# The causal clearing of the attention's diagonal blocks, moved from VectorE's product with a triangle to POOL's select on partition and position

## What is computed

```python
q, k, v = (split_heads(_layernorm(x) @ W + b) for W, b in qkv)   # (B, 16, T, 8)
scores = (l2norm(q) @ l2norm(k).T) * SCALE / TEMP
scores = where(tril(ones(T, T)), scores, -inf)                    # causal
x = x + 0.5 * (softmax(scores) @ v).merge() @ Wo + ...
```

## Time and profile before

| | us |
|---|---|
| median of 3 runs (lowest to highest) | 1459.83 (1456.45 to 1460.56) |
| the profiled execution's own time | 1460.59 |
| its span, first to last instruction | 1458.7 |
| PE / DVE / ACT / POOL busy | 1172.2 / 1118.2 / 804.6 / 659.2 |
| the attention: first to last exponential begins | 983.0 to 1426.0 |

### The profile page before, as it was taken

The page is one execution under the profiler, slowest core; times in us unless marked ns, Lnnn a source line. Parts: engine busy times, 40 slices in busy tenths (PEclk is TensorE's granted clock), DMA queues, the critical chain, the costliest instruction groups (busy, mean ns, idle before and its releaser), DMA issues. The chain is left out here.

```text
span 1458.7 us, 33100 instructions
## 1 busy us (share of the span) xinstructions
PE 1172.2 (80%) x11444; PEld 747.4 (51%) x11444; DVE 1118.2 (77%) x2557; ACT 804.6 (55%) x1477; POOL 659.2 (45%) x859
## 2 busy tenths in 40 slices
PE   7679954798898988998739994558987998899894
PEld 7369953455454545554618993444443543443333
DVE  6959963878888888899687995567778878876644
ACT  3768845455145235311347883127876777677881
POOL 2366633753773674365347663353233431521100
PEclk6789985698888898898658997568998999998996
DMA  9035340000000000000502342000000000000000
GB/s 283 11 99 171 89 59 15 26 5 5 20 9 1 23 9 2 2 2 2 197 4 77 90 89 44 15 15 14 2 23 6 19 23 1 16 8 8 1 16 8
DMA packets 55715, 55.11 MB, mean 38 GB/s; under 512 B 9882, under 2 KB 44484, under 8 KB 55556
## 3 DMA queue, kind: packets, MB, share of 16 engines
q1 hardware_dynamic: 46468, 34.37, 7.6%
q0 software_dynamic: 9088, 18.63, 5.7%
HBM read 32.26 MB, written 20.71 MB: 36 GB/s over the span
## 5 line engine op out<-in xcount | busy, mean ns | idle before, releaser
L2137 ACT ACTIVATE l_probs<-l_ps 128x1024 f32<-128x1024 f32 (+1 forms) x320 | 288.0, 946 | 106.6 <-PE l_ps L2023 104.7
L781 POOL DMA_INDIRECT ffn_yg<-y_rows,ffn_index x156 | 156.8, 1005 | 81.5 <-PE ffn_ps_t L796 37.8
L2042 PE MATMUL l_ps<-l_probs,l_vs 128*32 128x512 f32 (+3 forms) x1536 | 167.2, 525 | 28.0 <-DVE l_oTs L2370 16.2
L864 ACT ACTIVATE ffn_hT<-ffn_ps_h,experts_b1T,experts_scales 128x256 f32<-128x256 f32 x312 | 150.8, 562 | 30.5 <-PE ffn_ps_h L811 29.0
L263 POOL DMA_INDIRECT combine_og<-o_rows,combine_place x128 | 139.9, 1093 | 53.8 <-issue 31.4
L1307 PE MATMUL ssm_ps<-ssm_X,ssm_near 32*32 32x256 f32 x2048 | 136.8, 418 | 1.6 <-DVE ssm_Y L1750 1.6
L2361 DVE TENSOR_TENSOR l_probs<-l_probs,last_tri 128x256 f32<-128x256 f32 x256 | 102.5, 438 | 43.0 <-ACT l_probs L2137 41.2
L2023 PE MATMUL l_ps<-l_qkT 32*128 32x512 f16 (+3 forms) x768 | 110.6, 342 | 17.5 <-ACT l_probs L2137 15.4
L889 DVE SCALAR_TENSOR_TENSOR ffn_h<-ffn_hT,experts_scales,ffn_h 128x512 f16<-128x512 f32 x156 | 117.2, 751 | 5.5
L827 PE MATMUL ffn_ps_o<-experts_w,ffn_h 128*128 x624 | 112.8, 220 | 2.1 <-DVE ffn_h L889 1.9
L1549 POOL TENSOR_TENSOR ssm_u_out<-ssm_ysum,ssm_zx 128x256 f32<-128x256 f32 x32 | 69.0, 2157 | 97.7 <-DVE ssm_ysum L1761 97.6
(11 more groups left out here) (352 smaller groups left out, 2977.2 us busy)
## 6 DMA issues: line engine op xcount, KB each, us to landing
o_rows<-ffn_out_sb SPq DMA_DIRECT2D x78, 128.0 KB
y_rows<-ffn_y SPq DMA_DIRECT2D x8, 512.0 KB, 4.9
kept_w<-experts_w SPq DMA_DIRECT2D x16, 256.0 KB
experts_w<-kept_w SPq DMA_DIRECT2D x16, 256.0 KB, 5.9
ffn_yg<-y_rows,ffn_index POOLq DMA_INDIRECT x156
x_res<-in_L_attn_x SPq DMA_DIRECT2D x4, 512.0 KB, 6.1
prep_raw<-in_L_ffn_W SPq DMA_DIRECT2D x1, 2048.0 KB, 10.5
prep_raw<-in_L_ffn_W SPq DMA_DIRECT2D x8, 256.0 KB, 5.8
```

Of the source, the lines that this page charges most:

```text
L781: g_.indirect_dma_start(yg[:, i % RING, j].rearrange("p n d -> p (n d)"), None, w.y_rows.ap(), bass.IndirectOffsetOnAxis(ap=index[:, n:n + ...
L864: s.activation(hT[:, i % 2, c, :], ps_h[:, i % 2, c, :], ACT.Gelu, bias=w.b1T[:, bass.ds(e * HC + c, 1)], scale=SC[:, 6:7]).then_inc(h_rea ...
L2042: ins = t_.matmul(ps_o[VP * h:VP * h + VP, q0 % H:q0 % H + width], vs[:, s % 2, kb, h, :], probs[:, n % PSLOTS, i, at:at + width], start=( ...
L2137: s_.activation(probs[:, w % PSLOTS, i:i + n, 0:width], ps_s[w % 2][:, i:i + n, 0:width], ACT.Exp, scale=SCALE / (UNIT * UNIT)).then_inc(S ...
```

## The change

The products on DVE are taken out. In their place POOL gets a stream `masks` of the same form: the same due times, the same waits, the same semaphore. Its instruction is `affine_select` on the same 128x2x128 block, in place: an element stays where (position in the block) - (partition) >= 0 and becomes 0.0 elsewhere. It reads one tensor, where the product read two. The table `last_tri` is still loaded.

```diff
--- before.py
+++ after.py
@@ -2207,6 +2207,15 @@
                         nt = GROUP * (g % 2 + 1)
                         g_.tensor_copy(vs[:, s % 2, 0:nt, :, 0:VW], V[:, b % 2, 0:nt, hg]).then_inc(S["v_staged"], 1)
 
+                def masks():
+                    for w, (s, visits) in enumerate(cut.works):
+                        yield BEGIN + w + 1.2
+                        if cut.masks[w]:
+                            pool.wait_ge(S["e_done"], cut.exps_done[w])
+                        for i, n, at, _ in cut.masks[w]:
+                            p = probs[:, w % PSLOTS, i:i + n, at:at + P]
+                            g_.affine_select(p, p, [[0, n], [1, P]], ALU.is_ge, 0.0, base=0, channel_multiplier=-1).then_inc(S["m_done"], 1)
+
                 g_.memset(vs[:], 0.0).then_inc(S["zeroed"], 1)
                 pool.wait_ge(S["zeroed"], 1)
                 def fetch(g):
@@ -2214,7 +2223,7 @@
                         yield j
                         combine.fetch(pool, g * GROUP + j)
 
-                interleave([(0, values())] + [(L1_AT[g] - 9, fetch(g)) for g in range(GROUPS)] + [(0, uses.moving(("p", g), heads(g))) for g in range(GROUPS)] +
+                interleave([(0, masks()), (0, values())] + [(L1_AT[g] - 9, fetch(g)) for g in range(GROUPS)] + [(0, uses.moving(("p", g), heads(g))) for g in range(GROUPS)] +
                            [(at[g], norm(i, g)) for i, at in enumerate((L1_AT, P_AT, L2_AT)) for g in range(GROUPS)])
                 core.clear(pool)
 
@@ -2351,15 +2360,6 @@
                             ins = v.tensor_tensor(split[:, :, n, :, lo, :], qn, split[:, :, n, :, hi, :], ALU.subtract)
                     ins.then_inc(S["split_ready"], 1)
 
-                def masks():
-                    for w, (s, visits) in enumerate(cut.works):
-                        yield BEGIN + w + 1.2
-                        if cut.masks[w]:
-                            dve.wait_ge(S["e_done"], cut.exps_done[w])
-                        for i, n, at, _ in cut.masks[w]:
-                            p = probs[:, w % PSLOTS, i:i + n, at:at + P]
-                            v.tensor_tensor(p, p, tri[:].unsqueeze(1).broadcast_to([P, n, P]), ALU.mult).then_inc(S["m_done"], 1)
-
                 def close():
                     for s in range(cut.steps):
                         g, hg = s // 4, s % 4
@@ -2398,7 +2398,7 @@
                 chain.n += 3
                 v.tensor_copy(ident16[:], core.ident[:]).then_inc(S["const_ready"], 1)
                 dve.wait_ge(chain.sem, chain.n)
-                interleave([(0, masks()), (0, close())] + [(L1_AT[g] - 3, take_experts(g)) for g in range(GROUPS)] +
+                interleave([(0, close())] + [(L1_AT[g] - 3, take_experts(g)) for g in range(GROUPS)] +
                            [(0, uses.moving(("e", g), project(g))) for g in range(GROUPS)] +
                            [(0, uses.moving(("p", g), heads(g))) for g in range(GROUPS)] +
                            [(0, uses.moving((i, g), lora(i, g))) for i in range(2) for g in range(GROUPS)])
```

## The result

The changed kernel takes **1485.8 us** (median of 4 runs, 1484.12 to 1493.85) against 1459.76 of the kernel before (4 runs on the same chip, 1456.45 to 1460.56). The ratio is 1.0185, with a 95% interval of 1.0155 to 1.0215: 26.0 us slower. The profiled execution took 1484.17 us, span 1482.4, which is 23.6 above the profiled execution of before.

The account below looks back on a forecast made before the run. PE was taken to set the pace, though nowhere near full. Delays of 43 us less unused relief of 11.4 gave +31.6 on 1460.6, 1492.2; with the runs' median 0.8 lower, 1491 was said, 8 in 10 within 1472 to 1520.

Parts of the forecast that it names:

- Place and order: Gathers come late where a fetch or norm block precedes selects in POOL's queue: groups 0, 2, 4, less in 1, 3.
- the episodes: Gather delays behind POOL's fetch or norm blocks: 11.5 us in group 0, 10.8 in 2 and 4, 3.0 in 1 and 3.
- The relief: PE's waits for DVE that go: all 8.3 us for products, 8.1 of 16.2 for l_oTs; 11.4 left after odd groups.
- at most 24.5 us is to be won where PE visibly waits for DVE: PE's direct waits in the attention, 8.3 us for products and 16.2 for the copy l_oTs, bound the gain.
- 2 us for ten even steps and 2 for group 6: Small delays: 0.2 us per even step from a copy and two selects before the gather; group 6's norm block 2.
- POOL keeps up: Rival, 6%: fetch DMAs do not hold selects, or relief closes up PE's other streams; time 1436, or 1448 at half.
- No change: Rival, 5%: selects cost 0.43, PE makes up 3 us after each of five delays, all relief returns: +5.5, 1466.
- Selects held by DVE's reads: Rival, 17%: POOL's selects stand until DVE instructions end, costing 0.75 us each; time 1507.
- As slow as the comparison: Rival, 8%: a select on POOL takes 1.48 us, like its TENSOR_SCALAR with a comparison; time 1635.
- The gathers' new wait of some 40 us in pieces of up to 10: Sign: PE's gathers wait for POOL's selects in few, long pieces at the ends of groups 0, 2 and 4.
- Even groups 10 us longer each: Sign: groups 0, 2 and 4 each become about 10 us longer.
- Odd groups within 4 us: Sign: odd groups stay as long as before within 4 us.

Follow-up runs that it names:

- the version that shares by step: Changed kernel with 12 steps, where POOL also has a fetch, norm block or casts, back on DVE, fetches where they were: 1452.38 us, ratio 0.9933.
- the bare load: Changed kernel with selects writing a scratch tile from the triangle, no wait for exponentials, no gather waiting, diagonal blocks uncleared: 1447.62 us, ratio 0.9893.

## Why the prediction was right, and where it was not

The forecast was +31.6 us and the result is +26.0; 1485.8 lies in the range, and nearer to the forecast than to any rival. The mechanism of the loss was right. That the number is so near is in part luck: two terms of the sum were wrong by some 20 us each, and happened to cancel.

**Place and order: right.** The prediction named groups 0, 2 and 4 and a smaller loss in 1 and 3. The shifts show these, and one it had at nothing, steps 4 and 5 (3.9 us); the rows between copy and gather are gapless as laid out, POOL's wait before `l_vs` fell from 185.9 to 60.1 us, and no gather started before the rows ahead of its selects had ended. That moving five fetches takes away 29 us with selects and 5 with products shows the cause.

**Size of the episodes: too long in the even groups, too short in the odd.** Taken 11.5, 10.8, 10.8 and twice 3.0, 39.1 together; measured 9.2, 7.5, 7.6, 4.7 and 3.3, 32.3. The 24.0 us from the copy to the gather in group 2 were 21.0. Two things: a select was taken at 0.50 us, and has a median of 0.408 and, back to back, a pitch of (1.53 - 0.41) / 3 = 0.37, so 12 are 4.5 us, not 6.0; and the work ahead was taken at its durations of before, where a `norm` block took 3.4 us, and it now takes 3.0 (1130.49 to 1133.47). That no product of DVE runs beside it would fit; no run tests it. In group 1 the step's first late gather was 5.0 us late (1081.15, against 1068.79 + 7.4 of shift) for 5.5 forecast, and of this 1.5 came back in the next gather, not 2.5, to be lost again in the last.

**The relief: too small, for want of the clock.** The step "at most 24.5 us is to be won where PE visibly waits for DVE" failed. With the products gone altogether 36 us are won, 33 in the profiled executions. What the step counted was counted well: it used 16.4 us (11.4, and 5 set against the odd groups), and without products these waits fall by 17.1 and PE's idle time by 18.9. But PE's own instructions also take 14.1 us less, at a granted clock of 0.96 for 0.93. The prediction priced the clock only as a loss of 5 us in three even groups, and left it out of its sum; measured against before it is 6.6 us in the whole attention.

**What it leaves out: occupancy.** The sum had no term for 256 more instructions on POOL outside the five episodes but 2 us for ten even steps and 2 for group 6. It is 21 us, of which 8.8 of the 19.4 in the profiled attention are again PE's own time at a lower clock, and some 7 more for standing in the queue. With a relief of 36 in place of 16.4, the sum would have been 43 + 5 - 36 = +12. So an error of 20 us in the relief and one of 24 (28 less the 4 it had) in the occupancy stood on opposite sides, and with the 7 us by which the episodes were too long the sum came out 6 us off.

**The rivals.** *POOL keeps up*: it fell, the fetches do hold the selects; the version that shares by step shows that some of the time it spoke of, 10 us, is there when they don't. *No change*: its 15 us of making up after delays did not come, 1.1 us in step 7, as much in step 15 and 4.3 in groups 5 to 7 did. *Selects held by DVE's reads*: the mean is 0.454 us with a longest of 1.412, the bare load's is 0.421; these are 0.06 and 0.02 us above the least, where this rival had 0.25 above the forecast's 0.50. The Trainium skill (SBUF - State Buffer, Who interferes with whom) states that DVE and GpSimd lock each other out at a shared port pair. The rows agree in kind: it is seen less in the selects than on DVE's side, where `x_res` goes from 357 to 417 ns in the mean with the median unchanged, and to 346 where none stands beside a select. *As slow as the comparison*: excluded, 0.408 for 1.48.

The Trainium skill (GPSIMD Engine Reference, 4.1 Engine selection) has 2x for two inputs and roughly line rate for one. The select has one, and the trace agrees with the second half: 0.408 against DVE's 0.421, not 0.84.

**The signs named beforehand.** Selects of about 0.50: 0.45. The gathers' new wait of some 40 us in pieces of up to 10: 37.2, but up to 5.0. The prediction laid the whole delay of an episode on the 128x384 gather; in group 2 three gathers share it, with 2.28, 3.06 and 2.66 us. Even groups 10 us longer each: 7.5 to 9.2. Odd groups within 4 us: group 1 took 7.5 us more (+11.0 less +3.5), of which the prediction had 3.0; group 3 took 2.3 more. The clock in group 2: 0.74, where 0.80 was allowed for. No run holds PE's clock apart from its idle time: the busy time tells what the clock cost, not what made it fall.

## What to carry to other kernels

An idle engine is the sum of its gaps, and an instruction moved there pays for what stands ahead of it in that engine's order at the moment it is needed: find the long pieces of the queue (here eight indirect DMAs of 1.25 us each), and either move them or leave the work at these places where it was; shared by place, the same move gained 0.7% where moved whole it lost 1.9%. The waits that name a piece of work told here how much idle time its removal saves (17 us of waits went, 19 us of idle time), and not the whole gain: 33 us were won, 14 of them busy time of PE at a higher granted clock. So read the busy time and the clock of the limiting engine beside its waits. And run the kernel without the work, and with the work where nobody waits for it, and the two prices come apart. A correct total is no proof of its terms: here two errors of some 20 us cancelled.

## What the runs showed of the hardware that was not expected

- `affine_select` of 128x2x128 float32 in place on POOL: 397 ns at least, 408 in the median, 0.37 us apart when back to back; a DVE product of the same size with two inputs 406 and 421.
- POOL's `memset` of 128x352 takes 396 ns in the mean, about as long as a select of 128x256 (421 in the mean without waits).
- 256 selects that nobody waits for cost 21 us of 1460, and lengthen DVE's unchanged 2301 instructions by 15 us of busy time. Which DVE instruction is held depends on what stands beside it: `x_res` (two tensors read) took 1.1 us twice beside three selects back to back, and 353 ns at the longest where none of the 40 stood beside a select; `l_y` (one tensor) took up to 2.65 us beside a run of `memset`.
- The same 3456 instructions of PE in the attention are busy 388.46 us at a granted clock of 0.96, 397.28 at 0.94, 402.59 at 0.93 and 409.14 at 0.90. A gather of 16 products takes 1.07 us at full clock and 1.94 at half.
- From before to after, an even group (group 2) went in granted clock from 0.85 to 0.74 as PE's busy share fell from 84% to 70%; the odd group 1 went from 0.98 to 0.90 with the share at 89% both times (a share that counts the slower instructions too).
